# Gradient stages of a test-time-training layer: two gradient products by three float32r passes, silu and tanh in place of the sigmoid, steps written out

## The chip, the cores and the metric

One Trainium2 chip, one of its cores. The metric is the device time of one execution in microseconds, lower is better. Engines: TensorE (PE; PEld is its loading of weights), VectorE (DVE), ScalarE (ACT), GpSimd (POOL), SyncE (SP).

## The reference

Two transformer layers on 4096 tokens of width 128, each attention and a feed-forward part of experts. What the change touches is the second layer's "attention", a test-time-training layer: its parameters gate and val (128x512) and proj (512x128) are improved twice by a gradient over all tokens before they are used.

```python
def loss_fn(p):
    h = jax.nn.swish(k_ttt @ p['gate']) * (k_ttt @ p['val'])
    pred = h @ p['proj']
    return jnp.mean((pred - v_ttt) ** 2)
for _ in range(TTT_STEPS):                      # 2
    grads = jax.grad(loss_fn)(theta)
    theta = {kk: _muon_update(theta[kk], grads[kk]) for kk in theta}
```

With u = k gate, v = k val, s = silu(u), h = s v, dp = pred - v_ttt and dh = dp proj^T, the gradients are dproj = h^T dp, dval = k^T (dh s), dgate = k^T (dh v silu'(u)). silu'(u) = s + sigmoid(u) (1 - s) is called the slope here. `_muon_update` orthogonalizes each gradient (Newton-Schulz), after it is divided by its norm, so a constant factor on one gradient drops out up to rounding.

## The kernel before

The program runs stage by stage, with a barrier between: attention (to 1000 us or so), experts, projection, two rounds of gradient stage (`ttt_grads`) and `newton_schulz` (1323 to 1833 us), then output, routing and the last experts. `ttt_layer` calls the two in turn; both gradient stages run the same code.

`ttt_grads` walks over 32 tiles of 128 tokens. There is no scheduler: each engine's queue is written by hand, and a step n of every queue works on up to four tiles at once, tile n (u, v, s, h), m = n-1 (h transposed, pred, dp), l = n-2 (dp transposed, dh, dwp, du, dv) and o = n-3 (dwg, dwv). 35 steps in all. `steps` (L582) writes out the first four and the last three and makes a hardware loop of the others, four steps a turn. Semaphores count tiles, and every engine works its queue strictly in order.

- TensorE (L1520): transposition of dp (L1534), u and v (L1526, `three_passes`: hi x hi, hi x lo, lo x hi in float32r, which is float32 split into two parts), h transposed in four pieces (L1547), dh (L1526), dwp (L1555), pred (L1563), dwg (L1568), dwv (L1571). dwg, dwv and dwp gather over all tiles in PSUM. dwg and dwv are one float32 product of 128x512 each.
- ScalarE (L1576): the high part of dp^T (L1587), sigmoid of u (L1592), the copy of v (L1596), the copy of h^T (L1601).
- VectorE (L1605): the low part of dp^T (L1617), s = u sg (L1620), the slope in two operations (L1625, L1627), du (L1633), dv (L1634), h (L1639), dp (L1643).
- GpSimd (L1497): the keys of tile n, high and low part, copied from the big transposed array `turned` into `kTs` (L1504); ks, the keys of tile l by rows (L1509); w = slope v (L1515). In its queue the keys of tile n+1 stand behind w of tile n, which waits for VectorE.

The high and low parts of the three trained matrices are made at the start of each stage (L1578 on ScalarE, L1608 on VectorE), and TensorE starts when the last is done. In the trace the name c is the slope's buffer and valw, wv are val.

Of the kernel before, what the change touches and what calls it, by code (L numbers as in the profile page):

```python
# [1462 lines left out]
def ttt_grads(core, keep, grad_ps):  # L1463

# [5 lines left out]
    with ExitStack() as st:  # L1474
        sb = lambda name, shape: [core.sb(st, f"{name}{i}", shape) for i in range(2)]
        parts = lambda name, shape: [core.sb(st, f"{name}_{half}", shape, F32R) for half in ("hi", "lo")]
        kTs, ks = [parts(f"kTs{i}", [P, P]) for i in range(2)], sb("ks", [P, D])
# [4 lines left out]
        u_ps, v_ps, hT_ps, dh_ps = (core.ps(st, n, [P, HID]) for n in ("u_ps", "v_ps", "hT_ps", "dh_ps"))
        pred_ps = core.ps(st, "pred_ps", [P, 2, D])
        names = ("kT_staged", "k_staged", "u_done", "v_done", "sg_ready", "v_copied", "s_ready", "h_ready", "c_ready", "slope_ready", "w_ready",
                 "h_turned", "hT_ready", "pred_done", "dp_ready", "dp_turned", "dpT_ready", "dh_done", "du_ready", "dv_ready",
                 "dwp_done", "dwg_done", "dwv_done", "dpT_hi", "w_hi", "w_lo")
# [1229 lines left out]
```

## Time and profile before

| | us |
|---|---|
| median of 3 runs (lowest, highest) | 2140.37 (2134.65, 2141.48) |
| span of the profiled execution | 2178.4 |
| TensorE busy in it | 1866.1 (86%), 11556 matmuls |
| VectorE busy | 1597.3 (73%) |
| ScalarE busy | 1237.1 (57%) |
| GpSimd busy | 543.2 (25%) |
| mean granted TensorE clock | 0.921 |

The profile is one execution. For that one execution the span, from its first to its last instruction, is the only time given; it lies 38 us above the median of the runs. A timeline row gives the start in us from the span's start, the length in us, the engine, the line, the operation, the tile written and the tiles read, shapes, how many are merged (x8), and in brackets how long the engine sat idle before it and what ended that. Matmuls are pipelined: one row's length runs past the start of the next, so the time an operation costs TensorE is the distance from start to start. "MATMUL ... f32 x8" is four products, each recorded as two. float32r rows are shown with f32 as well; the tiles named _hi and _lo tell them apart.

### The profile page before, as it was taken

Reading aid. Unit: us, or ns where it says so; the run is one execution under the profiler, and the core shown is the slowest. Engines: PE = TensorE matmul, PEld = TensorE weight load, DVE = VectorE, ACT = ScalarE, POOL = GpSimd, SP = SyncE. Lnnn points to the kernel's source line nnn. Section 1 sums busy time; section 2 is a strip of 40 time slices with the busy share of each in tenths; the row PEclk is TensorE's granted clock in tenths of the full one; section 3 lists DMA queues with packets and bytes.
Section 4 is the critical chain, followed back from the end, with each engine's and each line's share of the span. In section 5 each row is a group of like instructions: output and inputs, shape, how many; then the busy total and the mean of one; then the engine's idle time right before and its main releaser. Section 6 shows DMA issues by size and latency. Waiting matters only on the chain. (4 is left out here: it accounts for less than half of the span.)

```text
span 2178.4 us, 35417 instructions
## 1 busy us (share of the span) xinstructions
PE 1866.1 (86%) x11556; PEld 1497.2 (69%) x11556; DVE 1597.3 (73%) x4179; ACT 1237.1 (57%) x2908; POOL 543.2 (25%) x602
## 2 busy tenths in 40 slices
PE   8999999999999999984766486999889998962772
PEld 6888888888888888873656344777667766741662
DVE  7999999999999999976546475777467765767524
ACT  6888888888888888864444363333233322440333
POOL 0111111111111111110544502444034421000472
PEclk9999999999999999996879587999999999985796
DMA  7000000000000000013554100000000000022354
GB/s 226 1 1 1 1 1 1 1 1 1 1 1 1 1 1 1 1 36 56 99 95 105 52 1 1 0 0 0 1 0 0 0 0 5 2 58 87 85 99 92
DMA packets 64893, 61.06 MB, mean 28 GB/s; under 512 B 10698, under 2 KB 54708, under 8 KB 64612
## 3 DMA queue, kind: packets, MB, share of 16 engines
q1 hardware_dynamic: 52276, 41.50, 6.5%
q0 software_dynamic: 10384, 16.59, 4.9%
q8 instruction: 82, 1.34, 0.3%
q10 hardware_dynamic: 2080, 1.05, 0.2%
q14 instruction: 71, 0.58, 0.1%
HBM read 40.12 MB, written 18.73 MB: 27 GB/s over the span
## 5 line engine op out<-in xcount | busy, mean ns | idle before, releaser
L461 DVE TENSOR_TENSOR probT<-turn_ps,probT 128x512 fp32r<-128x512 f32 x512 | 335.3, 686 | 63.3 <-ACT probT L359 63.2
L374 ACT ACTIVATE prob<-prob,negmax 128x512 f32<-128x512 f32 x512 | 375.4, 740 | 4.6 <-DVE negmax L455 4.6
L176 POOL TENSOR_TENSOR x<-x,scaled 128x512 f32<-128x512 f32 x128 | 166.8, 1303 | 802.1 <-DVE scaled L476 802.1
L455 DVE CUSTOM_DVE_ANT_0 prob<-score_ps,bias 128x512 f32<-128x512 f32 x512 | 341.2, 685 | 6.9 <-issue 1.1
L359 ACT CAST probT<-turn_ps 128x512 fp32r<-128x512 f32 x512 | 284.0, 598 | 21.7 <-PE turn_ps L259 21.7
L259 PE MATMUL turn_ps<-ident,prob 128*128 128x128 f32 x2048 | 266.2, 273 | 1.3 <-DVE probT L461 1.1
L276 PE MATMUL work_ps<-probT,val 128*128 128x512 f32 x1024 | 257.2, 393 | 0.1
L259 PEld LDWEIGHTS turn_ps<-ident,prob 128*128 128x128 f32 x2048 | 236.7, 140 | 28.2 <-DVE probT L461 3.4
L247 PE MATMUL score_ps<-k,q 64*128 64x512 f32 x1536 | 213.8, 410 | 2.4 <-DVE negmax L455 2.1
L276 PEld LDWEIGHTS work_ps<-probT,val 128*128 128x128 f32 x1024 | 187.5, 188 | 39.9 <-DVE probT L461 1.7
L247 PEld LDWEIGHTS score_ps<-k,q 64*128 64x128 f32 x1536 | 135.4, 185 | 47.3 <-issue 19.7
L1587 ACT CAST dpT_hi<-pred_ps 128x128 fp32r<-128x128 f32 x64 | 17.1, 267 | 234.1 <-PE pred_ps L1534 234.1
L291 PE MATMUL work_ps<-wo,ctxT 128*128 128x128 f32 x1024 | 146.0, 286 | 0.7 <-ACT ctxT L366 0.7
L291 PEld LDWEIGHTS work_ps<-wo,ctxT 128*128 128x128 f32 x1024 | 123.9, 191 | 26.3 <-issue 22.6
L1515 POOL TENSOR_TENSOR w<-c,vc 128x512 f32<-128x512 f32 x64 | 83.1, 1298 | 207.1 <-DVE c L1627 207.1
L366 ACT COPY ctxT<-work_ps 128x512 f32<-128x512 f32 x128 | 75.1, 587 | 84.5 <-PE work_ps L276 83.4
L374 ACT ACTIVATION_READ_ACCUMULATOR prob<-prob,negmax 128x1 f32 x512 | 106.1, 207 | 0.0
L476 DVE TENSOR_TENSOR scaled<-work_ps,inv 128x512 f32<-128x512 f32 x128 | 87.8, 686 | 2.7 <-PE work_ps L291 2.7
L1620 DVE TENSOR_TENSOR s<-u_ps,sg 128x512 f32<-128x512 f32 x64 | 44.3, 692 | 54.6 <-ACT sg L1592 54.6
L1504 POOL CAST kTs_hi<-turned_hi 128x128 fp32r (+1 forms) x64 | 45.5, 710 | 133.0 <-SPq L1474 133.0
L868 PE MATMUL h_ps<-xgT,own 128*128 128x128 f32 x320 | 60.6, 320 | 14.5 <-issue 14.5
L877 PE MATMUL y_ps<-w,hT 128*128 x320 | 60.6, 319 | 12.7 <-issue 7.2
(510 smaller groups left out, 4010.5 us busy)
## 6 DMA issues: line engine op xcount, KB each, us to landing
ew<-L_ffn_fc_weight SPq DMA_DIRECT2D x32, 256.0 KB
bias<-bias_line SPq DMA_DIRECT2D x16, 448.0 KB, 8.4
mid_rows<-row SPq DMA_DIRECT2D x40, 128.5 KB
last_rows<-row SPq DMA_DIRECT2D x40, 64.0 KB
rows_dram<-qk SPq DMA_DIRECT2D x1, 2304.0 KB, 18.5
x_rows<-x SPq DMA_DIRECT2D x4, 512.0 KB, 7.1
acc_dram<-zero POOLq DMA_DIRECT2D x1, 2048.0 KB, 16.3
out<-x SPq DMA_DIRECT2D x4, 512.0 KB
```

What stands on the lines that cost most here:

```text
L176: pool.tensor_tensor(mine, mine, scaled[a][:, :, :], ALU.add).then_inc(added, 1)
L247: mm = pe.matmul(score_ps[i % 2][a][:, :], q[p % 2][u][head(a), tile_of(i)], k[p % 2][v][head(a), :], start=(n == 0), stop=(n == 2))
L259: mm = pe.transpose(turn_ps[g % 2][:, tile_of(t)], prob[p % 2][a][:, t, tile_of(c)], ident[:, :])
L276: mm = pe.matmul(work[a][:, :], val[p // 2 % 2][:, c, p % 2 * 2 + a, :], probT[n][:, c, :], start=(c == 0 and n == 0), stop=(c == QT - 1 a ...
L291: mm = pe.matmul(work[1][:, tile_of(t)], ctxT[a][:, tile_of(t)], wo[:, 2 * (p % PAIRS) + a, :], start=True, stop=True)
L359: act.copy(probT[0][:, g % QT, :], turn_ps[g % 2][:, :]).then_inc(turned_hi, 1)
L366: act.copy(ctxT[a][:, :], work[a][:, :]).then_inc(ctx_ready, 1)
L374: act.activation(mine, mine, ACT.Exp, bias=negmax[p % 2][:, i, a:a + 1], scale=-1.0, accum_out=total[p % 4][:, i, a:a + 1]).then_inc(exp_d ...
L455: dve.tensor_tensor_reduce(prob[p % 2][a][:, i, :], score_ps[i % 2][a][:, :], bias[:, h, first:first + SEQ][:, ::-1], -1.0, 3.0e38, ALU.ad ...
L461: dve.tensor_tensor(probT[1][:, g % QT, :], turn_ps[g % 2][:, :], probT[0][:, g % QT, :].bitcast(F32), ALU.subtract).then_inc(turned_lo, 1)
L476: dve.tensor_tensor(scaled[a][:, :, :], work[1][:, :].rearrange("p (t d) -> p t d", t=QT), inv[p % 4][:, :, a:a + 1].to_broadcast([P, QT, ...
L1515: pool.tensor_tensor(w[r][:, :], c1[p][:, :], vc[p][:, :], ALU.mult).then_inc(w_ready, 1)
```

## The change

Only `ttt_grads` and one constant of `newton_schulz` change.

1. dwg and dwv are computed by `three_passes` over high and low parts of ks, du and dv. New work: the parts of ks (a cast and a subtraction on GpSimd), the casts of du and dv on ScalarE, the low part of du on VectorE (one step later), the low part of dv on GpSimd.
2. ScalarE computes s = silu(u) and th = tanh(u/2) from PSUM; sigmoid and VectorE's product for s are gone. The slope becomes (s + 1) - (s - 1) th, which is twice silu'(u) (two operations, as before, one step later); the factor 2 on dgate is taken out in `newton_schulz`.
3. The keys' parts are read by TensorE in place; GpSimd's two copies are gone.
4. No hardware loop: all 35 steps are written out. w has two buffers in place of four, and VectorE's order in a step is dpT_lo, du_lo, slope, slope, du, dv, dp, h.
5. u of tile n waits for silu and tanh of tile n-1, v of tile n for the copy of v of tile n-1.

```diff
         @block.gpsimd
-                    for k in range(2):
-                        pool.tensor_copy(kTs[p][k][:, :], kT[k][:, bass.ds(n * P, P)]).then_inc(kT_staged, 1)
+            def keys(l):
+                p = l % 2
+                if l >= 2:
+                    pool.wait_ge(k_lo, l - 1)
+                pool.tensor_tensor(ks[p][:, :], qk[:, l, D:2 * D], keep["shift"][:, D:2 * D], ALU.add).then_inc(k_summed, 1)
+                pool.wait_ge(k_summed, l + 1)
+                if l >= 2:
+                    pool.wait_ge(dwv_done, l - 1)
+                pool.tensor_copy(ks_parts[p][0][:, :], ks[p][:, :]).then_inc(k_hi, 1)
+                pool.wait_ge(k_hi, l + 1)
+                pool.tensor_tensor(ks_parts[p][1][:, :], ks[p][:, :], ks_parts[p][0][:, :].bitcast(F32), ALU.subtract).then_inc(k_lo, 1)
...
+            def low_dv(l):
+                p = l % 2
+                pool.wait_ge(dv_hi, l + 1)
+                if l >= 2:
+                    pool.wait_ge(dwv_done, l - 1)
+                pool.tensor_tensor(dv_parts[p][1][:, :], dv[p][:, :], dv_parts[p][0][:, :].bitcast(F32), ALU.subtract).then_inc(dv_lo, 1)
+
+            for n in range(STEPS):
+                if live(n - 2):
+                    keys(n - 2)
+                if live(n - 1):
+                    weigh_slope(n - 1)
+                if live(n - 2):
+                    low_dv(n - 2)
...
         @block.tensor
-                    pe.wait_ge(kT_staged, 2 * (n + 1))
-                    if again(n, 1):
+                    keys = [half[:, columns(n)] for half in kT]
+                    if n >= 1:
                         pe.wait_ge(s_ready, n)
+                        pe.wait_ge(th_ready, n)
+                    three_passes(u_ps[:, :], keys, wg).then_inc(u_done, 1)
+                    if n >= 1:
                         pe.wait_ge(v_copied, n)
-                    three_passes(u_ps[:, :], kTs[p], wg).then_inc(u_done, 1)
-                    three_passes(v_ps[:, :], kTs[p], wv).then_inc(v_done, 1)
+                    three_passes(v_ps[:, :], keys, wv).then_inc(v_done, 1)
...
-                    pe.matmul(dwg_ps[:, :], ks[q][:, :], du[q][:, :], start=isinstance(o, int) and o == 0,
-                              stop=isinstance(o, int) and o == TILES - 1, skip_group_check=True).then_inc(dwg_done, 1)
+                    pe.wait_ge(k_lo, o + 1)
+                    pe.wait_ge(du_lo, o + 1)
+                    three_passes(dwg_ps[:, :], whole(ks_parts[o % 2]), du_parts[o % 2], **edges).then_inc(dwg_done, 1)
+                    pe.wait_ge(dv_lo, o + 1)
+                    three_passes(dwv_ps[:, :], whole(ks_parts[o % 2]), dv_parts[o % 2], **edges).then_inc(dwv_done, 1)
...
         @block.scalar
-                    act.activation(sg[p][:, :], u_ps[:, :], ACT.Sigmoid).then_inc(sg_ready, 1)
+                    act.activation(s[r][:, :], u_ps[:, :], ACT.Silu).then_inc(s_ready, 1)
+                    if n >= 2:
+                        act.wait_ge(c_ready, n - 1)
+                    act.activation(th[p][:, :], u_ps[:, :], ACT.Tanh, scale=0.5).then_inc(th_ready, 1)
...
+                if live(l):
+                    p = l % 2
+                    act.wait_ge(du_ready, l + 1)
+                    if l >= 2:
+                        act.wait_ge(dwg_done, l - 1)
+                    act.copy(du_parts[p][0][:, :], du[p][:, :]).then_inc(du_hi, 1)
+                    act.wait_ge(dv_ready, l + 1)
+                    if l >= 2:
+                        act.wait_ge(dwv_done, l - 1)
+                    act.copy(dv_parts[p][0][:, :], dv[p][:, :]).then_inc(dv_hi, 1)
...
         @block.vector
-                    dve.tensor_tensor(s[r][:, :], u_ps[:, :], sg[p][:, :], ALU.mult).then_inc(s_ready, 1)
+                if live(o):
+                    p = o % 2
+                    dve.wait_ge(du_hi, o + 1)
+                    if o >= 2:
+                        dve.wait_ge(dwg_done, o - 1)
+                    dve.tensor_tensor(du_parts[p][1][:, :], du[p][:, :], du_parts[p][0][:, :].bitcast(F32), ALU.subtract).then_inc(du_lo, 1)
...
+                    dve.scalar_tensor_tensor(c1[p][:, :], s[r][:, :], -1.0, th[p][:, :], ALU.add, ALU.mult).then_inc(c_ready, 1)
+                    dve.wait_ge(c_ready, m + 1)
+                    dve.scalar_tensor_tensor(c1[p][:, :], s[r][:, :], 1.0, c1[p][:, :], ALU.add, ALU.subtract).then_inc(slope_ready, 1)
...
-                act.activation(first[m], x_ps[m], ACT.Copy, scale=grad_scale).then_inc(copied, 1)
+                act.activation(first[m], x_ps[m], ACT.Copy, scale=grad_scale * (0.5 if m == 0 else 1.0)).then_inc(copied, 1)
```

The order of instructions, at the places that matter. TensorE, the end of a step, from pred on; before:

```order
L1563 MATMUL pred_ps<-proj,hT_460 128x128 x4
L1568 MATMUL dwg_ps<-du_468,ks_434 128x512
L1571 MATMUL dwv_ps<-dv_470,ks_434 128x512
L1534 MATMUL pred_ps<-ident,dp_462 128x128
L1536 ISA
L1526 MATMUL u_ps<-wg_hi,kTs_hi 128x512
```

and now (`turned` is the array with the transposed keys):

```order
L1578 MATMUL pred_ps<-proj,hT_458 128x128 x4
L1539 MATMUL dwg_ps<-du_hi,ks_hi 128x512
L1539 MATMUL dwg_ps<-du_lo,ks_hi 128x512
L1539 MATMUL dwg_ps<-du_hi,ks_lo 128x512
L1539 MATMUL dwv_ps<-dv_hi,ks_hi 128x512
L1539 MATMUL dwv_ps<-dv_lo,ks_hi 128x512
L1539 MATMUL dwv_ps<-dv_hi,ks_lo 128x512
L1547 MATMUL pred_ps<-ident,dp_460 128x128
L1539 MATMUL u_ps<-wg_hi,turned_hi 128x512
```

Two products became six passes; nothing else moved on TensorE. GpSimd, one step, before:

```order
L1504 COPY kTs_hi<-turned_hi 128x128
L1504 COPY kTs_lo<-turned_lo 128x128
L1509 TENSOR_TENSOR ks_434<-qk,shift 128x128
L1515 TENSOR_TENSOR w_458<-c_446,vc_444 128x512
```

and now:

```order
L1501 TENSOR_TENSOR ks_430<-qk,shift 128x128
L1505 CAST ks_hi<-ks_430 128x128
L1507 TENSOR_TENSOR ks_lo<-ks_430,ks_hi 128x128
L1514 TENSOR_TENSOR w_455<-c_445,vc_443 128x512
L1521 TENSOR_TENSOR dv_lo<-dv_468,dv_hi 128x512
```

and VectorE's step now:

```order
L1641 TENSOR_TENSOR dpT_lo<-pred_ps,dpT_hi 128x128
L1647 TENSOR_TENSOR du_lo<-du_465,du_hi 128x512
L1654 SCALAR_TENSOR_TENSOR c_445<-s_449,th_441 128x512
L1656 SCALAR_TENSOR_TENSOR c_445<-s_449,c_445 128x512
L1661 TENSOR_TENSOR du_466<-dh_ps,w_456 128x512
L1664 TENSOR_TENSOR dv_468<-dh_ps,s_448 128x512
L1667 TENSOR_TENSOR dp_459<-pred_ps,v 128x128
L1673 TENSOR_TENSOR h_454<-s_450,vc_444 128x512
```

GpSimd has a second 128x512 operation in each step; VectorE has eight operations as before, h now last. ScalarE, from the start of the stage, now:

```order
L1591 CAST wpT_hi<-projT 128x512
L1605 ACT_TABLE_LOAD
L1605 ACTIVATE s_447<-u_ps 128x512
L1608 ACTIVATE th_441<-u_ps 128x512
L1612 COPY vc_443<-v_ps 128x512
L1605 ACTIVATE s_448<-u_ps 128x512
L1608 ACTIVATE th_442<-u_ps 128x512
L1612 COPY vc_444<-v_ps 128x512
L1617 COPY hT_457<-hT_ps 128x512
```

One table load stands ahead of the first silu, where one stood ahead of the first sigmoid; no other follows before the square root of Newton-Schulz.

## Rows read from the trace of the kernel before

**Rows 1.** Windows: length, busy of PE, PEld, DVE, ACT, POOL, clock, DMA share, GB/s
```profile
1323.00:1336.00 13.00, 5.83 (x13) 4.04 (x14) 5.16 (x8) 4.72 (x7) 2.64 (x5) 0.50 0.00 1
...
1396.00:1426.00 30.00, 30.00 (x169) 23.12 (x168) 22.10 (x40) 9.73 (x20) 12.91 (x19) 1.00 0.00 0
```
**Rows 2.** Timeline of one middle step, TensorE (start, length, operation, shapes)
```profile
1401.93 0.27 PE L1534 MATMUL pred_ps<-ident,dp 128*128 128x128 f32 x1
...
1402.75 0.39 PE L1526 MATMUL v_ps<-wv_hi,kTs_hi 128*128 128x512 f32 x1
...
1403.44 0.60 PE L1547 MATMUL hT_ps<-ident,h 128*128 128x128 f32 x4
...
1403.79 0.48 PE L1526 MATMUL dh_ps<-wpT_hi,dpT_hi 128*128 128x512 f32 x1
1404.11 0.39 PE L1526 MATMUL dh_ps<-wpT_lo,dpT_hi 128*128 128x512 f32 x1
...
1405.46 1.06 PE L1563 MATMUL pred_ps<-proj,hT 128*128 128x128 f32 x8
...
1406.35 1.02 PE L1568 MATMUL dwg_ps<-du,ks 128*128 128x512 f32 x2
...
1408.07 0.27 PE L1534 MATMUL pred_ps<-ident,dp 128*128 128x128 f32 x1
```
**Rows 3.** Timeline of the same step, the other engines
```profile
1402.31 0.46 POOL L1509 TENSOR_TENSOR ks<-qk,shift 128x128 f32<-128x128 f32 x1 [0.45 <-PE dwv_ps L1571]
...
1402.70 0.29 DVE L1617 TENSOR_TENSOR dpT_lo<-pred_ps,dpT_hi 128x128 fp32r<-128x128 f32 x1 [1.03 <-ACT dpT_hi L1587]
1402.95 0.60 ACT L1592 ACTIVATE sg<-u_ps 128x512 f32<-128x512 f32 x1 [0.36 <-PE u_ps L1526]
...
1404.15 0.59 ACT L1601 COPY hT<-hT_ps 128x512 f32<-128x512 f32 x1
...
1405.80 1.27 POOL L1515 TENSOR_TENSOR w<-c,vc 128x512 f32<-128x512 f32 x1 [3.04 <-DVE c L1627]
...
1406.84 0.78 DVE L1639 TENSOR_TENSOR h<-s,vc 128x512 f32<-128x512 f32 x1
1407.02 0.75 POOL L1504 CAST kTs_hi<-turned_hi 128x128 fp32r x1
...
1407.55 0.28 DVE L1643 TENSOR_TENSOR dp<-pred_ps,v 128x128 f32<-128x128 f32 x1
```
**Rows 4.** Timeline of the start of the first gradient stage
```profile
1323.79 0.62 ACT L1578 CAST wg_hi<-gate 128x512 fp32r<-128x512 f32 x1 [5.23 <-PEq L59]
...
1324.32 0.61 ACT L1578 CAST wv_hi<-valw 128x512 fp32r<-128x512 f32 x1
1324.44 0.69 DVE L1608 TENSOR_TENSOR wg_lo<-gate,wg_hi 128x512 fp32r<-128x512 f32 x1 [5.09 <-ACT wg_hi L1578]
...
1325.47 1.28 ACT L1592 ACT_TABLE_LOAD   x1
...
1328.08 0.60 ACT L1592 ACTIVATE sg<-u_ps 128x512 f32<-128x512 f32 x1 [1.33 <-PE u_ps L1526]
...
1330.77 0.68 DVE L1639 TENSOR_TENSOR h<-s,vc 128x512 f32<-128x512 f32 x1
1330.94 1.64 POOL L1515 TENSOR_TENSOR w<-c,vc 128x512 f32<-128x512 f32 x1 [6.60 <-DVE c L1627]
...
1333.10 0.79 PE L1526 MATMUL u_ps<-wg_hi,kTs_hi 128*128 128x512 f32 x1 [3.78 <-POOL kTs_lo L1504]
...
1340.02 0.48 PE L1534 MATMUL pred_ps<-ident,dp 128*128 128x128 f32 x1 [0.38 <-DVE dp L1643]
```
**Rows 5.** Timeline of GpSimd at the span's start
```profile
1.25 0.28 POOL L165 TENSOR_SCALAR_AFFINE_SELECT ident<-ident 128x128 f32<-128x128 f32 x1 [0.24 <-POOL ident L163]
```
**Rows 6.** Timeline of the end of the second gradient stage
```profile
1785.03 0.68 DVE L1634 TENSOR_TENSOR dv<-dh_ps,s 128x512 f32<-128x512 f32 x1
...
1787.69 1.02 PE L1571 MATMUL dwv_ps<-dv,ks 128*128 128x512 f32 x2
```

More of the change, by code:

```diff
@@ L1476, in ttt_grads @@
         parts = lambda name, shape: [core.sb(st, f"{name}_{half}", shape, F32R) for half in ("hi", "lo")]
-        kTs, ks = [parts(f"kTs{i}", [P, P]) for i in range(2)], sb("ks", [P, D])
+        two_parts = lambda name, shape: [parts(f"{name}{i}", shape) for i in range(2)]
+        ks, ks_parts = sb("ks", [P, D]), two_parts("ks", [P, D])
         wg, wv, wpT = (parts(n, [P, HID]) for n in ("wg", "wv", "wpT"))
-        sg, vc, c1 = (sb(n, [P, HID]) for n in ("sg", "vc", "c1"))
-        s, h, w = ([core.sb(st, f"{n}{i}", [P, HID]) for i in range(RING)] for n in "shw")
@@ L1481, in ttt_grads @@
-        hT, dp, dpT, du, dv = sb("hT", [P, HC, P]), sb("dp", [P, D]), [parts(f"dpT{i}", [P, P]) for i in range(2)], sb("du", [P, HID]), sb("dv", [P, HID])
+        th, vc, c1 = (sb(n, [P, HID]) for n in ("th", "vc", "c1"))
+        s, h = ([core.sb(st, f"{n}{i}", [P, HID]) for i in range(RING)] for n in "sh")
+        w = sb("w", [P, HID])
+        hT, dp, dpT = sb("hT", [P, HC, P]), sb("dp", [P, D]), two_parts("dpT", [P, P])
+        du, dv, du_parts, dv_parts = sb("du", [P, HID]), sb("dv", [P, HID]), two_parts("du", [P, HID]), two_parts("dv", [P, HID])
@@ L1490, in ttt_grads @@
+        (k_summed, k_hi, k_lo, u_done, v_done, s_ready, th_ready, v_copied, h_ready, c_ready, slope_ready, w_ready,
+         h_turned, hT_ready, pred_done, dp_ready, dp_turned, dpT_hi, dpT_ready, dh_done, du_ready, dv_ready,
+         du_hi, dv_hi, du_lo, dv_lo, dwp_done, dwg_done, dwv_done, w_hi, w_lo) = (core.sem(n) for n in names)
         block = st.enter_context(nc.Block())
-        run = lambda eng, step: steps(eng, step, TILES, 3, RING, RING)
-        live = lambda n: not isinstance(n, int) or 0 <= n < TILES
@@ L1522, in _, with three_passes @@
             pe.wait_ge(w_lo, len(trained))
-            def three_passes(to, left, right):
+            def three_passes(to, left, right, start=True, stop=True, across=False):
                 for k, (i, j) in enumerate(PASSES):
-                    mm = pe.matmul(to, left[i][:, :], right[j][:, :], start=(k == 0), stop=(k == 2))
+                    mm = pe.matmul(to, left[i], right[j][:, :], start=start and k == 0, stop=stop and k == 2, skip_group_check=across)
                 return mm
-            def step(n, r):
-                p, q = r % 2, 1 - r % 2
+            whole = lambda two: [half[:, :] for half in two]
+            for n in range(STEPS):
                 m, l, o = n - 1, n - 2, n - 3
@@ L1578, in _ @@
                 act.copy(hi[:, :], whole[:, :]).then_inc(w_hi, 1)
-            def step(n, r):
-                p, q = r % 2, 1 - r % 2
+            for n in range(STEPS):
                 m, l = n - 1, n - 2
```

123 lines of the change are left out of this document (52 added, 71 removed).

## Prediction

> **What bounds the kernel now.** The busy shares of the page are averages over stages with different limits, so the table by stage comes first [rows 1]: in 30 us from the middle of a gradient stage TensorE is busy for 30.00 at a granted clock of 1.00 (its 2.4 GHz level), VectorE for 22.10, GpSimd for 12.91, ScalarE for 9.73. TensorE sets the pace there. The timeline of one step, TensorE alone, shows it [rows 2]: from one transposition of dp (1401.93) to the next (1408.07) are 6.14 us, and each operation starts where the one before it ends. The reader should see a belt: transposition and u 0.82 (to 1402.75), v 0.69, transpositions of h 0.35, dh and dwp 1.67, pred 0.89, dwg and dwv 1.72; together 6.14. The other engines in the same step [rows 3] have gaps: the dp that TensorE takes at 1408.07 is ready at 1407.83, and w and the copy of h^T lie well ahead of their readers.
>
> **TensorE, steady state.** The change replaces dwg and dwv, float32 operations that take 1.72 together (1406.35 to 1408.07 [rows 2]), by three float32r passes each. v is three such passes of 128x512 in 0.69 (1402.75 to 1403.44), so 0.23 each. The first pass behind a float32 operation took 0.32 (dh, 1403.79 to 1404.11); six passes take 6 x 0.23 = 1.38, or 1.47 if that 0.09 is paid once, behind pred. The gain is 0.25 to 0.34 a step. I take the middle, 0.30, since dwg also stands behind a float32 operation but its weights are small and may be loaded during pred: a step takes 5.84. Of a stage's steps three fill and three drain, counted below; 29 steps x 0.30 = 8.7 us in a stage.
>
> **What must stay hidden for that.** I lay a step of 5.84 out from the durations of the rows, time 0 being the transposition of dp.
> ScalarE: silu can start where sigmoid does now (1.02) and ends at 1.62; neither a row for silu nor for tanh exists, the bounds are a copy of the same size from PSUM (0.59) and the cast from SBUF (0.62), and I take the 0.60 of sigmoid. Tanh starts 0.53 later (the spacing of the casts wg_hi and wv_hi [rows 4]), then the copies of v and h^T, the last one to 3.25. pred may start at 3.53, as in the belt: 0.3 in hand, where today there are 0.7 (copy ends at 1404.74, pred starts at 1405.46 [rows 2, 3]). The casts of du and dv, 0.62 each as wg_hi, follow du and dv, to 5.3.
> VectorE: the product for s leaves (0.69, as long as its neighbours), du_lo comes (0.69, as wg_lo<-gate,wg_hi [rows 4]). dpT_lo goes to 0.97 as now, du_lo to 1.8, the two slope operations to 3.4, du to 4.0, dv to 4.6, dp when pred is done, 4.66 to 4.94, h to 5.6. TensorE wants dp at 5.84: 0.9 in hand.
> GpSimd: the two copies of keys leave (the first takes 0.75 [rows 3]), as TensorE reads them in place. The cast and the low part of ks come (0.28 as the select of 128x128 [rows 5], 0.46 as ks), and the low part of dv. No row has a two-input float32r output on GpSimd: the lower bound is w's 1.27 for as many elements, the upper one w's 1.64 under VectorE's h [rows 4]; I take 1.27, which is the same shape undisturbed. Sum 0.46 + 0.28 + 0.46 + 1.27 + 1.27 = 3.74, and twice 0.24 between operations that depend on each other [rows 5]: 4.2 of 5.84. dv_lo is ready near 6.7, and its reader, dwv, stands at 5.84 + 5.2: hidden with 4 us in hand. If that cover were gone, each step would grow by what it is late.
> The shared port: GpSimd and VectorE hold each other off when VectorE has two inputs in SBUF. h is issued 1.04 behind w and takes 0.78 in place of 0.68; kTs_hi, issued under h, takes 0.75 [rows 3] where the select of its size takes 0.28 [rows 5]; w takes 1.64 in place of 1.27 when issued 0.17 behind h [rows 4]. So w keeps VectorE out for 1.04 + 0.10 = 1.14, and h keeps GpSimd out for 0.17 + 0.37 = 0.54. In the new step du_lo, both slope operations and h are of that kind, 4 x 0.54 = 2.16. Laid out: ks 0.73 to 1.19, its cast behind du_lo at 1.63, its low part behind the first slope operation, 2.38 to 2.84, w behind the second, 3.5 to 4.8, under du and dv, which read PSUM, h from 4.87, dv_lo from 5.4 to 6.7, 0.83 into the next step, when its ks is due. It closes, with a few tenths in hand. I take 0; below 0 is excluded, since TensorE's belt is full, and above it stands rival (c).
>
> **Filling and draining.** Today u of tile 1 stands at 1333.10, because its staged keys were queued on GpSimd behind w of tile 0 [rows 4]. With keys in place it waits for tanh of tile 0: 1328.08 + 0.53 + 0.60 = 1329.2, 3.9 earlier, with the same work behind it up to the first transposition of dp (1340.02 today). The clock was 0.50 here [rows 1]. If it rises at the same moment as today, the work that moves forward is done more slowly and 1 is given back; if it rises as early as the work does, 2 are won. Range 3 to 6, taken 4.0. At the end, du and dv of the last tile get casts and low parts: dv at 1785.03 + 0.68, cast 0.62, GpSimd 1.3, three passes 0.69, to 1788.4; today's last dwv starts at 1787.69 and needs 0.86, to 1788.55 [rows 6]. No change. Casts, low parts and the table load at the start of a stage stay.
>
> **Sum.** 2 x (8.7 + 4.0) = 25.4 us. The profiled execution has a span of 2178.4, so it should show 2153. The median of the runs lies 38 lower (2140.4), and no row ties that difference to these stages, so the gain is carried over whole: 2140.4 - 25.4 = 2115.
>
> **Rivals.**
> (a) Half of the 0.30 is refilled, because the copy of h^T comes later than planned and pred waits, and a step takes 6.0: 2 x (29 x 0.14 + 4) = 16, 2124. For it: the 0.3 in hand there is the smallest of all. Chance 0.14.
> (b) All of it is refilled and a step stays at 6.14: only the filling is won, 8, which gives 2132. Chance 0.10.
> (c) Slower: the port. Should dv_lo get in ahead of h (its input is there at 5.3, h starts at 4.87, so half a microsecond decides), GpSimd keeps VectorE out for 1.14 in every step, besides 0.33 + 0.15 + 0.33 for the operations on ks (each 0.13 less than its length, as w). VectorE's loop is 0.67 from the transposition to the start of dpT_lo, 0.2 + 0.6 + 0.7 + 0.6 + 0.6 + 0.6 + 0.3 from there through dp, some 4.4 with the way back; with 1.95 of exclusion 6.3, with part of h in it 6.6. GpSimd's own sum says alike: 4.2 + 2.16 = 6.3 with nothing overlapped. From 6.37 a step the kernel is slower by over 0.3%; at 6.6 it is 2 x (29 x 0.46 - 4) = +19: 2159. Against it: the layout closes. Chance 0.12, slower GpSimd operations included. The Trainium skill has this as a rule, in "SBUF — State Buffer", section "SBUF: two separate sides": of a GpSimd operation and a VectorE operation with two SBUF inputs the one that starts first has the shared pair for the whole instruction, and the other blocks. The trace agrees (0.10 on h, 0.47 on kTs_hi).
> (d) The change does not do what it says: silu and tanh share no function table, and each tile pays two loads, 64 x 2 x 1.28 = 164 [rows 4]: 2279. Against it: the program has one load a stage, ahead of the first silu. Chance 0.02. The Trainium skill ("ScalarE: Activation LUTs", section "Table sets: the hidden batching unit") lists tanh beside exp and beside sigmoid, names no set for silu, and says to group calls by set. The instruction order shown above says that here they share one.
>
> **How the numbers follow.** My forecast has 0.62: with 0.25 a step and 3 of filling it gives 20.5 (2120), with 0.34 and 6 it gives 31.7 (2109). About 0.3% (6.4 us) is what a measurement can tell from no change, so faster is below 2134. Faster: 0.62 + 0.14 + half of (b) = 0.81. Same: the rest of (b) and a little of (c), 0.07. Slower: 0.12. The range runs from 2107 (2 below the best end, for the scatter of the runs, which is 7 wide) through (a) and (b) to 2135; (c) and (d) are outside.
>
> **What would show it.** Right: TensorE busy 30.00 of 30.00 in mid-stage, transpositions of dp 5.8 to 5.9 apart, six passes of 0.23 where 1.72 stood, the last dwv some 25 us ahead of 1787.69, one table load a stage, u of tile 1 about 3 us behind u of tile 0. Wrong, by step: TensorE idle ahead of pred for h^T (a); idle ahead of the transposition for dp, with h or du_lo far above 0.69, or w and dv_lo above 1.3 (c); u of tile 1 still late (filling). If steps are 5.8 apart and the time has not fallen, the loop written out costs elsewhere.

## The result and the profile after

| | before | after |
|---|---|---|
| median (lowest, highest), 4 runs each | 2137.51 (2132.53, 2141.48) | 2105.76 (2104.53, 2107.28) |
| span of the profiled execution | 2178.4 | 2102.6 |
| length of the two gradient stages in it | 212.8, 211.9 | 195.2, 195.0 |
| mean granted TensorE clock | 0.921 | 0.933 |

The ratio is 0.9854, 95% interval 0.9839 to 0.9869: 31.7 us less, where the prediction had 25.4. (The kernel before has one run more than when the prediction was made, and its median came 2.9 lower.) A stage's length is taken here from its first cast to ScalarE's first reading of dwg. The two stages are 34.4 shorter together (424.65 to 390.23). The spans differ by 75.8, but 43.1 of that lies ahead of the first gradient stage (its first cast at 1280.69, 1323.79 before [rows 4]), in code that the change leaves alone: in the trace of before, GpSimd idles 38.8 us at the experts' gathers for VectorE, in the one after 8.1, which is 30.7 of the 43.1. That is no part of the gain, and below only stage lengths and ratios are compared between runs.

The page of the changed kernel (busy time and share, instructions):

```profile
PE 1828.0 (87%) x11684; PEld 1508.8 (72%) x11684; DVE 1603.9 (76%) x4179; ACT 1338.7 (64%) x3100; POOL 705.4 (34%) x666
```

The windows that answer to [rows 1], start and middle of a stage:

```profile
1280.00:1293.00 13.00, 8.32 (x33) 6.12 (x34) 5.77 (x11) 7.55 (x14) 2.96 (x4) 0.72 0.00 1
1353.00:1383.00 30.00, 30.00 (x187) 26.19 (x186) 23.55 (x42) 18.17 (x36) 27.00 (x27) 1.00 0.00 1
```

TensorE still sets the pace, with no gap. GpSimd rose from 12.91 to 27.00 of 30 and is the next in line. At the start the clock is 0.72 where it was 0.50. One middle step, TensorE, answering to [rows 2]:

```profile
1360.13 0.27 PE L1547 MATMUL pred_ps<-ident,dp 128*128 128x128 f32 x1
...
1363.65 1.06 PE L1578 MATMUL pred_ps<-proj,hT 128*128 128x128 f32 x8
...
1364.46 0.48 PE L1539 MATMUL dwg_ps<-du_hi,ks_hi 128*128 128x512 f32 x1
...
1364.78 0.39 PE L1539 MATMUL dwg_ps<-du_lo,ks_hi 128*128 128x512 f32 x1
...
1365.01 0.39 PE L1539 MATMUL dwg_ps<-du_hi,ks_lo 128*128 128x512 f32 x1
...
1365.92 0.27 PE L1547 MATMUL pred_ps<-ident,dp 128*128 128x128 f32 x1
```

From transposition to transposition are 5.79 (6.14 before). The six passes take 1.46 (1364.46 to 1365.92) in place of 1.72, and pred 0.81 in place of 0.89. The other engines in the same step, answering to [rows 3]:

```profile
1360.94 0.68 DVE L1647 TENSOR_TENSOR du_lo<-du,du_hi 128x512 fp32r<-128x512 f32 x1
1360.96 0.99 POOL L1501 TENSOR_TENSOR ks<-qk,shift 128x128 f32<-128x128 f32 x1
1361.13 0.60 ACT L1605 ACTIVATE s<-u_ps 128x512 f32<-128x512 f32 x1 [0.43 <-PE u_ps L1539]
...
1361.54 0.95 DVE L1654 SCALAR_TENSOR_TENSOR c<-s,th 128x512 f32<-128x512 f32 x1
1361.63 0.59 ACT L1608 ACTIVATE th<-u_ps 128x512 f32<-128x512 f32 x1
...
1362.57 0.61 ACT L1617 COPY hT<-hT_ps 128x512 f32<-128x512 f32 x1
...
1363.50 1.27 POOL L1514 TENSOR_TENSOR w<-c,vc 128x512 f32<-128x512 f32 x1
...
1364.74 0.29 DVE L1667 TENSOR_TENSOR dp<-pred_ps,v 128x128 f32<-128x128 f32 x1 [0.33 <-PE pred_ps L1578]
...
1364.95 0.68 DVE L1673 TENSOR_TENSOR h<-s,vc 128x512 f32<-128x512 f32 x1
...
1365.15 1.64 POOL L1521 TENSOR_TENSOR dv_lo<-dv,dv_hi 128x512 fp32r<-128x512 f32 x1 [0.38 <-ACT dv_hi L1627]
```

The copy of h^T ends at 1363.18, 0.47 ahead of pred; dp is there at 1365.03, 0.89 ahead of its transposition. GpSimd and VectorE pay for their shared port in what they have to spare: ks 0.99 (0.46 alone), the slope's first operation 0.95 (0.69 alone), dv_lo 1.64 (least 1.27). The start of the first stage, answering to [rows 4]:

```profile
1282.37 1.28 ACT L1605 ACT_TABLE_LOAD   x1
...
1283.29 0.80 PE L1539 MATMUL u_ps<-wg_hi,turned_hi 128*128 128x512 f32 x1 [8.56 <-DVE wpT_lo L1633]
...
1285.47 0.59 ACT L1608 ACTIVATE th<-u_ps 128x512 f32<-128x512 f32 x1
...
1286.21 0.77 PE L1539 MATMUL u_ps<-wg_hi,turned_hi 128*128 128x512 f32 x1
1286.26 0.59 ACT L1612 COPY vc<-v_ps 128x512 f32<-128x512 f32 x1 [0.20 <-PE v_ps L1539]
...
1286.77 0.62 PE L1539 MATMUL u_ps<-wg_lo,turned_hi 128*128 128x512 f32 x1
...
1287.69 0.40 PE L1539 MATMUL v_ps<-wv_lo,turned_hi 128*128 128x512 f32 x1
```

u of tile 1 stands 2.92 behind u of tile 0, with no idle time of TensorE ahead of it, and the copy of v of tile 0 starts only then. At about 1287 the passes go from 0.43 apart to 0.23: the clock rose from 0.50 to 1.00 3.8 after u of tile 0; before, it rose some 14.5 after.

### The profile page after: what moved, and what is told of

The parts are those of the page before. It is cut to its first block and busy times, and to the rows that moved or that the text cites. A ratio compares the mean times of both kernels' runs of the same rounds, so it can differ in the third digit from the quotient of the medians.

```text
span 2102.6 us, 35597 instructions
## 1 busy us (share of the span) xinstructions
PE 1828.0 (87%) x11684; PEld 1508.8 (72%) x11684; DVE 1603.9 (76%) x4179; ACT 1338.7 (64%) x3100; POOL 705.4 (34%) x666
## 3 DMA queue, kind: packets, MB, share of 16 engines
q10 hardware_dynamic: 2080, 1.05, 0.2%
## 5 line engine op out<-in xcount | busy, mean ns | idle before, releaser
L1521 POOL TENSOR_TENSOR dv_lo<-dv,dv_hi 128x512 fp32r<-128x512 f32 x64 | 102.1, 1596 | 27.4 <-ACT dv_hi L1627 27.4
L1623 ACT CAST du_hi<-du 128x512 fp32r<-128x512 f32 x64 | 39.6, 619 | 51.3 <-DVE du L1661 51.3
L1570 PEld LDWEIGHTS dwp_ps<-dp,h 128*128 128x128 f32 x512 | 67.2, 191 | 5.6
L1578 PE MATMUL pred_ps<-proj,hT 128*128 128x128 f32 x512 | 67.8, 275 | 2.0 <-ACT hT L1617 2.0
L1570 PE MATMUL dwp_ps<-dp,h 128*128 128x128 f32 x512 | 67.6, 275 | 0.0
```

Of the source, the lines that this page charges most:

```text
L1521: pool.tensor_tensor(dv_parts[p][1][:, :], dv[p][:, :], dv_parts[p][0][:, :].bitcast(F32), ALU.subtract).then_inc(dv_lo, 1)
L1570: mm = pe.matmul(dwp_ps[:, c, :], h[l % RING][:, columns(c)], dp[l % 2][:, :], start=l == 0 and c == 0, stop=l == TILES - 1, skip_group_ch ...
```

## The experiments

They ran on four chips: b_out, b_keys, a_f32 and a_swap, where the kernel before took 2136.91 (19 runs); b_keys_h, a_sig, a_pool1 and a_pool2 (2143.59, one run); b_keys_v, a_vwait, a_warm and a_start (2178.12, 7 runs); b_keys_vd, after_5 and a_start_5 (2188.14, 9 runs). On the last two the first gradient stage begins 42 to 55 us later than in the trace of after, with GpSimd waiting at the gathers named above (43.0 us in after_5). So the table gives what the traces show of the stages themselves, first / second stage, in us: the length; u of tile 1 and the transposition of dp of tile 0 (T0) and of tile 1 (T1), counted from u of tile 0; and the mean step of tiles 4 to 28. The changed kernel itself, on two chips, differs by 0.7 and 0.8 in its stages (after, after_5), 0.6 and 0.4 of it ahead of T0; a difference of that size between two chips' traces is not a finding.

| | length | u1 | T0 | T1 | step |
|---|---|---|---|---|---|
| before | 212.8 / 211.9 | 6.71 / 6.52 | 13.63 / 12.52 | 20.08 / 19.18 | 6.143 |
| after | 195.2 / 195.0 | 2.92 / 2.73 | 8.02 / 7.79 | 13.05 / 12.83 | 5.793 |
| b_out | 212.4 / 212.7 | 6.70 / 6.70 | 12.60 / 12.45 | 19.88 / 20.03 | 6.141 |
| b_keys | 208.2 / 208.3 | 3.69 / 3.70 | 9.66 / 9.67 | 15.66 / 15.69 | 6.140 |
| b_keys_h | 210.1 / 208.2 | 3.69 / 3.70 | 10.58 / 9.67 | | 6.146 |
| b_keys_v | 206.9 / 206.4 | 3.06 / 2.40 | 8.32 / 7.71 | 14.32 / 13.71 | 6.143 |
| b_keys_vd | 205.6 / 205.3 | 3.06 / 2.73 | 7.99 / 7.66 | 13.28 / 12.95 | 6.133 |
| a_f32 | 205.2 / 205.2 | 2.91 / 2.88 | 7.81 / 7.77 | 12.84 / 12.80 | 6.133 |
| a_swap | 196.4 / 196.0 | | | | 5.793 |
| a_sig | 208.4 / 208.5 | 3.05 | 7.98 / 8.08 | 13.5 | 6.190 |
| a_pool1 | 195.1 / 195.0 | | | | 5.793 |
| a_pool2 | 203.2 / 203.4 | | | | 6.042 |
| a_vwait | 199.2 / 198.8 | 3.70 / 3.69 | 10.58 / 10.58 | 16.56 / 16.17 | 5.803 |
| a_warm | 195.1 / 194.5 | 2.90 / 2.24 | 7.56 / 6.86 | 12.59 / 11.89 | 5.793 |
| a_start | 193.7 / 193.6 | 2.85 / 2.92 | 7.46 / 7.54 | 12.49 / 12.56 | 5.793 |
| after_5 | 195.9 / 195.9 | 2.91 / 2.91 | 8.62 / 8.22 | 13.64 / 13.25 | 5.793 |
| a_start_5 | 194.1 / 193.9 | 2.89 / 2.81 | 7.83 / 7.42 | 12.86 / 12.45 | 5.793 |

### Parts alone and parts undone

**b_out**: the kernel before, its loop written out.

```diff
-        run = lambda eng, step: steps(eng, step, TILES, 3, RING, RING)
+        run = lambda eng, step: [step(n, n % RING) for n in range(TILES + 3)]
```

> The kernel before with the hardware loop written out and nothing else. Theory A: turning the loop costs nothing that a full TensorE shows, so steps 6.14, a stage 212 to 213, the time within 3 us of the kernel before. Rival (the loop's branches cost something every four steps, which was part of the gain): a stage 1 to 5 us shorter.

Measured 2135.18, ratio 0.9987 (0.9977 to 0.9997), stages and step as before. The medians are 1.7 us apart, a little beyond the noise, but the gradient stages, where the loop stood, are no shorter: there it cost nothing.

**b_keys**: b_out with the keys read in place.

```diff
-                    for k in range(2):
-                        pool.tensor_copy(kTs[p][k][:, :], kT[k][:, bass.ds(n * P, P)]).then_inc(kT_staged, 1)
...
-                    pe.wait_ge(kT_staged, 2 * (n + 1))
```

> The kernel before with two things of the change alone: the steps are written out, and TensorE reads the keys in place (GpSimd's two copies and the wait for them are gone). Theory A (the filling was mis-sized: TensorE starts tile 1 at once, so it is busier and its clock rises early): u of tile 1 stands 3 to 3.5 us behind u of tile 0 in place of 6.7, the second transposition of dp 6 to 7 us earlier than in the kernel before counted from u of tile 0, steps still 6.14, a stage 206 in place of 212.8, the time 12 to 14 us below the kernel before. Rival B (the surplus came from the steps, or from silu and tanh on ScalarE, and the keys only win the 4 us that were taken): second transposition 3.5 to 4 earlier, a stage 209, the time 8 lower.

2128.94, ratio 0.9965 (0.9952 to 0.9978): 8.0 us, 4.0 a stage, what the prediction took for it, and no more. So rival B held; theory A's early start did not come, as u of tile 1 stands at 3.69 and not at 3 to 3.5. Against b_out on the same chip, which has the loop written out too, the medians are 6.2 apart and the stages in the traces 8.7.

**a_f32**: the changed kernel with dwg and dwv in float32 again, without casts and low parts.

```diff
-                    three_passes(dwg_ps[:, :], whole(ks_parts[o % 2]), du_parts[o % 2], **edges).then_inc(dwg_done, 1)
+                    pe.matmul(dwg_ps[:, :], ks[o % 2][:, :], du[o % 2][:, :], start=o == 0, stop=o == TILES - 1, skip_group_check=True).then_inc(dwg_done, 1)
```

> The changed kernel with dwg and dwv as float32 products again (no casts and low parts of ks, du, dv); silu, tanh, keys in place and the order of VectorE stay. Theory A: steps of 6.14 again, filling as in the changed kernel, a stage 195.2 + 31 x 0.345 = 206, the time 21 us above the changed kernel and some 13 below the kernel before. Rival B: if the 0.345 a step has another source than the passes, steps stay near 5.8 to 5.9.

2125.36, ratio 0.9944 (0.9928 to 0.9961), step 6.133. The passes are worth 0.34 a step and 10 a stage. But a_f32 is also 3.05 a stage shorter than b_keys, 2.8 to 2.9 of it ahead of T1. The prediction has no term for that; b_keys_h and the group "The missing filling" look for it.

**a_swap**: dv and its cast ahead of du, so that dv_lo gets its input before h starts, as rival (c) wanted.

```diff
                     dve.wait_ge(dh_done, l + 1)
-                    dve.wait_ge(w_ready, l + 1)
-                    dve.tensor_tensor(du[p][:, :], dh_ps[:, :], w[p][:, :], ALU.mult).then_inc(du_ready, 1)
                     if l >= 2:
                         dve.wait_ge(dv_lo, l - 1)
                     dve.tensor_tensor(dv[p][:, :], dh_ps[:, :], s[l % RING][:, :], ALU.mult).then_inc(dv_ready, 1)
+                    dve.wait_ge(w_ready, l + 1)
+                    dve.tensor_tensor(du[p][:, :], dh_ps[:, :], w[p][:, :], ALU.mult).then_inc(du_ready, 1)
...
```

> The changed kernel with dv ahead of du on VectorE and its cast ahead on ScalarE, so that dv_lo on GpSimd is ready to go 0.6 earlier, ahead of h. Theory A (VectorE has 0.9 in hand and h is needed late): h takes up to 1.8 in place of 0.68, steps stay 5.79 to 5.85, the time within 4 us of the changed kernel. Rival (c) of the prediction (the port decides when dv_lo gets in ahead of h): steps 6.3 to 6.6, a stage 16 to 25 us longer, the time 30 to 50 us above the changed kernel.

2103.26, ratio 0.9843 (0.9824 to 0.9862), step 5.793. The two tiles in its trace (duration ns least/median/most):

```profile
L1521 POOL TENSOR_TENSOR dv_lo<-dv,dv_hi x64: 1268/1291/1848, 1296.4 to 1710.1; 128x512 fp32r<-128x512 f32 x64
...
L1673 DVE TENSOR_TENSOR h<-s,vc x64: 683/1409/1829, 1287.2 to 1700.8; 128x512 f32<-128x512 f32 x64
```

The collision happens: h takes 1.41 where it took 0.68, and dv_lo no longer waits (1.29 for 1.64). It costs no step anything; VectorE's spare time takes it up (26.86 busy of 30 in mid-stage, for 23.55). The stages are 1.2 and 1.0 longer all the same: 0.7 of that lies behind the last transposition of dp, where TensorE idles 1.17 for du_lo, now made later, and the rest ahead of T0. Rival (c)'s place was right and its price was not.

### What is next in line

**b_keys_h**: b_keys with h of tile n ahead of the slope's operations on VectorE.

```diff
                 if live(n):
+                    dve.wait_ge(v_copied, n + 1)
+                    if again(n, RING):
+                        dve.wait_ge(dwp_done, n - RING + 1)
+                    dve.tensor_tensor(h[r][:, :], s[r][:, :], vc[p][:, :], ALU.mult).then_inc(h_ready, 1)
```

> The kernel with keys in place and steps written out (b_keys), and VectorE's h moved ahead of the two slope operations. Theory A (what the prediction left out of the filling is that h of a tile no longer stands behind two slope operations, 1.4 us): first transposition of dp 8.2 to 8.4 behind u of tile 0 in place of 9.7, a stage 206 to 207 in place of 208.2, steps 6.14. Rival B (the filling got shorter because silu on ScalarE makes s at once, without VectorE): first transposition stays within 0.5 of 9.7, a stage 208.

2129.0 in one run, the stages no shorter than b_keys's; the first is 1.9 longer, and the clock rises only 12.6 after u of tile 0 in it. That theory of the missing 3 us fell.

**a_sig**: the changed kernel with the sigmoid on ScalarE and the product for s on VectorE again.

```diff
-                    act.activation(s[r][:, :], u_ps[:, :], ACT.Silu).then_inc(s_ready, 1)
-                    act.activation(th[p][:, :], u_ps[:, :], ACT.Tanh, scale=0.5).then_inc(th_ready, 1)
+                    act.activation(th[p][:, :], u_ps[:, :], ACT.Sigmoid).then_inc(th_ready, 1)
...
+                    dve.tensor_tensor(s[n % RING][:, :], u_ps[:, :], th[n % 2][:, :], ALU.mult).then_inc(s_ready, 1)
```

> The changed kernel with sigmoid and VectorE's product for s again (s just ahead of h, at the end of VectorE's step), the slope in its old form; passes, keys and casts as in the change. Theory A: u of tile 1 waits for s of VectorE and stands 3.7 behind u of tile 0 in place of 2.9, the filling is 1 to 2 us longer, steps stay 5.79 to 5.85 because VectorE's ninth operation fits, a stage 196 to 198. Rival B (silu and tanh are needed for the step: VectorE has nine operations, 5.0 us, and up to 1.2 of waiting for the port): steps of 6.0 to 6.4, a stage 202 or more.

**a_pool1** and **a_pool2**: the changed kernel with one more copy a step on GpSimd that nobody reads, 128x128 and 128x512.

```diff
+                    pool.wait_ge(more_done, n - 1)
+                    pool.tensor_copy(more[n % 2][:, :], wp[:, :, :].rearrange("p a b -> p (a b)")).then_inc(more_done, 1)
```

> The changed kernel with one more copy of 128x128 on GpSimd in each step, behind w. GpSimd is busy for 5.3 of 5.79 in the changed kernel, waiting for the port included; the copy takes 0.3 to 0.65. Theory A (TensorE sets the step, GpSimd is next with 0.5 in hand): steps 5.79 to 5.85. Rival (c) of the prediction (the port ring is already at its limit): steps 6.1 or more.

> The changed kernel with one more copy of 128x512 on GpSimd in each step, behind w. Theory A: GpSimd's queue, with 0.5 in hand, becomes the longest and each step grows by the copy's length less 0.5: steps 6.0 to 6.5, a stage 7 to 22 us longer. Rival: the copy is hidden, steps 5.79, because waiting for the port shrinks by as much.

One run each: a_sig 2126.04, a_pool1 2105.33, a_pool2 2123.07. The middle window of a_sig, then of a_pool2:

```profile
1353.00:1383.00 30.00, 29.39 (x177) 24.12 (x176) 29.66 (x44) 15.35 (x30) 23.69 (x25) 1.00 0.00 1
```

```profile
1353.00:1383.00 30.00, 29.81 (x180) 24.67 (x179) 29.83 (x40) 17.39 (x35) 29.28 (x31) 1.00 0.00 1
```

With the product for s back on VectorE, VectorE is busy 29.66 of 30, a step takes 6.19, and the whole gain of the passes is gone, as rival B had it (u of tile 1 stood at 3.05, not at theory A's 3.7). So in a steady step silu and tanh save nothing on a path of their own; they make the room in which the low part of du is free. Another place for that product in VectorE's queue was not tried. In a_pool2 a copy that takes 0.60 undisturbed, and 1.08 in a middle step, lengthens the step by 0.25: GpSimd had under a microsecond to spare (a_pool1's copy fits in), and VectorE is busy 29.83 with the same eight operations. du, dv and dp, which read PSUM, are as long as before; the four with both inputs in SBUF now wait longer for the port:

```profile
1359.36 1.72 POOL L1522 TENSOR_TENSOR dv_lo<-dv,dv_hi 128x512 fp32r<-128x512 f32 x1
...
1359.86 1.77 DVE L1657 SCALAR_TENSOR_TENSOR c<-s,th 128x512 f32<-128x512 f32 x1
```

The slope's first operation takes 1.77, for 0.95 in the changed kernel and 0.69 alone. That is the ring of rival (c): it closes one 128x512 copy beyond this change.

### The missing filling

**b_keys_v** and **a_vwait**: one wait of TensorE moved, forward in b_keys and back in the changed kernel. In b_keys_v

```diff
                         pe.wait_ge(s_ready, n)
-                        pe.wait_ge(v_copied, n)
                     three_passes(u_ps[:, :], here, wg).then_inc(u_done, 1)
+                    if again(n, 1):
+                        pe.wait_ge(v_copied, n)
```

and in a_vwait

```diff
                         pe.wait_ge(th_ready, n)
+                        pe.wait_ge(v_copied, n)
                     three_passes(u_ps[:, :], keys, wg).then_inc(u_done, 1)
-                    if n >= 1:
-                        pe.wait_ge(v_copied, n)
```

> b_keys with one wait of TensorE moved: the wait for the copy of v of tile n-1 stands ahead of v of tile n, no longer ahead of u. Theory A (part of the 3 us a stage that b_keys still lacks in filling is this wait: TensorE idles 0.77 ahead of u of tile 1, and the clock rises later): no gap there, u of tile 1 within 3.0 of u of tile 0 (3.69 in b_keys), passes at 0.23 by 5 us behind u of tile 0, first transposition of dp at 8.0 to 8.8 (9.66), stage 206 to 207 (208.2). The rest of the 3 us would be VectorE's queue ahead of dp. Theory B (the wait is nothing, since sigmoid and s of tile 0 are late as well): u of tile 1 stays at 3.4 or more, stage 208.2. Steps 6.14 by both.

> The changed kernel with the wait for the copy of v of tile n-1 put back ahead of u of tile n. Theory A: u of tile 1 some 0.7 later (3.6 behind u of tile 0, 2.9 in the changed kernel), the clock rises later, first transposition of dp at 9 to 9.7 (8.0), stage 196.3 to 197.2 (195.1). Theory B: stage within 0.3 of 195.1. Step 5.79 by both.

One run each, 2170.77 and 2150.8. b_keys_v is 1.2 and 1.9 a stage shorter than b_keys; a_vwait is 4.0 and 3.7 longer than after and 3.3 and 2.9 longer than after_5, more than any theory expected. TensorE at the start of a_vwait, the wait's gap first, then pred of tile 0:

```profile
1329.51 0.77 PE L1539 MATMUL u_ps<-wg_hi,turned_hi 128*128 128x512 f32 x1 [0.77 <-ACT vc L1611]
...
1333.93 2.08 PE L1577 MATMUL pred_ps<-proj,hT 128*128 128x128 f32 x8 [0.67 <-ACT hT L1616]
```

and its windows from u of tile 0 on, then the changed kernel's:

```profile
1325.80:1329.80 4.00, 3.22 (x7) 2.15 (x8) 0.33 (x1) 2.04 (x4) 0.00 (x0) 0.50 0.00 0
1329.80:1333.80 4.00, 3.46 (x10) 2.37 (x9) 1.66 (x3) 2.18 (x4) 2.08 (x4) 0.50 0.02 4
1333.80:1337.80 4.00, 3.48 (x12) 3.00 (x13) 1.48 (x4) 0.35 (x2) 0.36 (x1) 0.50 0.00 0
1337.80:1341.80 4.00, 4.00 (x27) 3.54 (x26) 2.28 (x4) 2.88 (x6) 1.29 (x1) 0.91 0.00 0
```

```profile
1283.20:1287.20 4.00, 3.91 (x9) 2.67 (x10) 0.28 (x2) 2.12 (x4) 0.00 (x0) 0.50 0.00 0
1287.20:1291.20 4.00, 2.72 (x17) 2.06 (x15) 1.98 (x5) 2.05 (x4) 2.00 (x4) 0.99 0.00 0
```

The wait itself is 0.77 of idle time (3.22 busy of 4.00, 3.91 without it). The rest is the clock: it stays at 0.50, its 1.2 GHz level, through twelve us instead of four, pred takes 2.08 where the same eight products take 1.16 in the changed kernel's first step, and T0 comes at 10.58 in place of 8.02. How late the clock rises varies: from u of tile 0 it is 11.9 and 12.7 in a_vwait's two stages, 7.7 and 8.1 in those of b_keys with the same gap, and 3.5 to 6.0 without the gap (after, after_5, a_f32, a_swap, a_pool1, a_pool2). So in each pair of kernels the wait costs more than its 0.77, but how much more is not settled by single runs.

**b_keys_vd**: b_keys_v with VectorE's dp ahead of h, as in the changed kernel.

> b_keys_v with VectorE's dp ahead of h, as the changed kernel has it. Theory A (what b_keys_v still lacks is dp queued behind h in filling: in it dp of tile 1 starts a microsecond behind the end of pred): transposition of dp of tile 1 about 5.3 behind that of tile 0 (6.0 in b_keys_v), stage 205 to 205.9, the level of a_f32 (205.2). Theory B (h comes too late for its transposition, or the order of the two is nothing): 6.0 and 206.4 to 207.0 as in b_keys_v. Steps 6.14 by both.

2169.08 in one run. The stages are 1.3 and 1.05 shorter. Of that 0.71 lies between T0 and T1, which go from 6.00 to 5.29 apart in both stages; the rest is smaller than what chips differ by. VectorE at that point, in b_keys_v and in b_keys_vd:

```profile
1338.71 0.78 DVE L1635 TENSOR_TENSOR h<-s,vc 128x512 f32<-128x512 f32 x1
...
1339.41 0.28 DVE L1639 TENSOR_TENSOR dp<-pred_ps,v 128x128 f32<-128x128 f32 x1
```

```profile
1344.78 0.28 DVE L1634 TENSOR_TENSOR dp<-pred_ps,v 128x128 f32<-128x128 f32 x1
1344.97 0.68 DVE L1639 TENSOR_TENSOR h<-s,vc 128x512 f32<-128x512 f32 x1
```

In the middle of a stage this order costs next to nothing, since dp is early (steps of 6.143 and 6.133); in filling TensorE waits for dp. With both edits a stage is 205.3 to 205.6, against 205.2 in a_f32: the account closes within 0.4, less than one kernel's stages differ between chips. The traces show where most of that is, in the wait for dp ahead of T1, in b_keys_vd and then in a_f32:

```profile
1345.11 0.33 PE L1529 MATMUL pred_ps<-ident,dp 128*128 128x128 f32 x1 [0.64 <-DVE dp L1634]
```

```profile
1301.96 0.33 PE L1539 MATMUL pred_ps<-ident,dp 128*128 128x128 f32 x1 [0.38 <-DVE dp L1643]
```

In b_keys_vd VectorE works without a pause from the product for s through the slope, du and dv to dp; in a_f32, where silu has made s and the slope is a step later, it idles ahead of dp for pred. That is 0.26 a stage for item 2 of the change, read from the traces and not made alone by an edit.

**a_warm** and **a_start**: the changed kernel with the start of the stage altered. a_warm puts 14 transpositions of the identity ahead of TensorE's first wait; a_start puts 8, and lets u of tile 0 wait for gate's low part alone.

```diff
+            keep_busy(pe, hT_ps, ident, 8)
-            pe.wait_ge(w_lo, len(trained))
...
+                    if n == 0:
+                        pe.wait_ge(w_lo, 1)
                     three_passes(u_ps[:, :], keys, wg).then_inc(u_done, 1)
```

> The changed kernel with 14 transpositions of the identity on TensorE at the start of each gradient stage, while it waits for the parts of the trained matrices; their result is never read. If the clock's level at the start is what filling still costs: passes of u of tile 0 at 0.23 instead of 0.43, stage 1 to 1.5 shorter (193.6 to 194.1), time 2 to 3 lower than the changed kernel's, 2103. If the level falls again before u of tile 0, or filling is bound by the chain of small operations rather than by TensorE: stage 194.8 to 195.2, 2105.5.

> The changed kernel with 8 such transpositions, and with the one wait for all low parts of the trained matrices taken apart: u of tile 0 waits for gate's, v for val's, dh for proj's. u of tile 0 can start about 1.2 earlier. If both count: stage 1.2 to 2.5 shorter (192.6 to 193.9), time 2101 to 2103.5. If the sigmoid-side chain behind v of tile 0 sets the filling: stage 194.5 or more, 2105.

a_warm: 2145.14, ratio 0.9842 (0.9817 to 0.9866); a_start: 2146.44, ratio 0.9849 (0.9822 to 0.9876). The first four us of a_warm's first stage from u of tile 0 on, after 2.9 us of transpositions with no gap behind them:

```profile
1329.80:1333.80 4.00, 4.00 (x13) 2.70 (x12) 0.33 (x1) 1.82 (x5) 0.00 (x0) 0.62 0.00 0
```

Here the passes of u of tile 0 stay 0.43 apart, which theory had at 0.23: that was a miss. In its second stage they are at 0.23 from the start, though TensorE idled 0.86 behind the transpositions:

```profile
1565.22 0.50 PE L1540 MATMUL u_ps<-wg_hi,turned_hi 128*128 128x512 f32 x1 [0.86 <-DVE wpT_lo L1634]
1565.56 0.40 PE L1540 MATMUL u_ps<-wg_lo,turned_hi 128*128 128x512 f32 x1
1565.80 0.40 PE L1540 MATMUL u_ps<-wg_hi,turned_lo 128*128 128x512 f32 x1
```

In the changed kernel, too, the second stage begins with the clock at 1.00, which Newton-Schulz left; but TensorE idles up to its first pass, and the level falls to 0.50 within half a microsecond of it (in after_5 it had fallen 1.7 ahead of it). In no run without transpositions did it last through the first microsecond. With them it stayed at 1.00 in the second stage of a_warm and of a_start_5, and fell in that of a_start. So a filler may keep the level, and did not raise it ahead of the first passes in any first stage. a_warm's stages are 0.1 to 0.5 shorter than those of after, 0.8 to 1.4 shorter than those of after_5, so whether the filler is worth anything in all stays open. a_start's, where u of tile 0 starts 1.0 and 1.2 earlier, are 1.4 to 2.3 shorter than either. To see whether that reaches the total, both kernels ran beside each other on another chip:

> The changed kernel again, as the control for the run beside it on the same chip. Ratio to the kernel before 0.984 to 0.987.

> a_start again, beside the changed kernel on one chip. Its stages are 1.4 shorter in the trace, so 2.8 less than the control if nothing is given back between the stages (ratio 0.0013 lower); if Newton-Schulz or the barrier gives it back: within 1 of the control.

after_5: 2151.57 (2146.80 to 2153.71), ratio 0.9831 (0.9811 to 0.9852): 36.6 us less than before where the first chip had 31.7, and a ratio just below the 0.984 expected. a_start_5: 2150.24 (2149.57 to 2153.41), ratio 0.9827 (0.9807 to 0.9847). The stages are 1.8 and 2.0 shorter in the trace, the medians differ by 1.3 and the runs overlap: no version was shown to beat the changed kernel.

## Where the prediction held, and which step failed

- **The bound** (TensorE's belt, 30.00 of 30.00) and **what stays hidden**: right. The layout held nearly in every place: the copy of h^T 0.47 ahead of pred where 0.3 was forecast, dp 0.89 in hand where 0.9 was, dv_lo behind h, GpSimd with a few tenths to spare (a_pool1, a_pool2). Rivals (a) and (b) did not come about.
- **Steady state**, "I take the middle, 0.30": it was 0.35, just beyond the upper end of 0.34. Where the prediction weighed whether 0.09 would be paid behind pred, the trace shows both: the first pass takes 0.32 to the next, as dh's did, and pred becomes 0.08 shorter when a float32r pass follows it. The whole of pred, dwg and dwv went from 2.61 to 2.27. That the weights of dwg are small was no reason for less: dwg's first pass took what dh's did. By this 0.05 x 29 x 2 = 2.9 us were missed.
- **Filling**: "the same work behind it up to the first transposition of dp" is the step that failed. The start of u of tile 1 was right to 0.1 (3.8 earlier, 3.9 forecast), and b_keys alone gave the 4.0 a stage taken. But the changed kernel's filling gave 7.2 (7.6 and 6.7 from before to a_f32): T0 came 5.6 and 4.7 earlier, and T1 another 1.4 and 1.6. The other 3 are two items of the change's description that the prediction priced at nothing without saying so: the wait for the copy of v, moved from u to v (1.2 and 1.9 a stage in b_keys_v), and VectorE's order, dp ahead of h (1.3 and 1.05 in b_keys_vd). Of the 0.4 and 0.15 left, the wait ahead of T1 shows 0.26 for item 2, s ready without VectorE; the remainder is within what chips differ by. The term's range of 3 to 6 took the clock as the only unknown and so was too narrow.
- **The sum** by traces: keys 8.2, the moved wait 3.1, dp ahead of h 2.4, the rest of the filling 0.6, passes 20.1, together 34.4. It closes because each term is the difference of two traces; b_keys_v and b_keys_vd ran once each, and on other chips. The medians' 31.7 is below that; its interval, 28 to 34, takes it in just about, and after_5's 36.6 lies above, so which is nearer isn't settled. The result, 2105.76, lies 1.2 below the range.
- **Drain**, no change: right, from the last transposition of dp to the reading of dwg are 6.56 before and 6.57 after, though TensorE idles 0.21 there for dv_lo.
- **Rival (c)**: its collision was made in a_swap and costs no step anything at this load; in a_pool2, one copy later, a step grows. Its step from which the kernel is slower, 6.37, should be 6.39 by its own formula. The Trainium skill ("SBUF — State Buffer", section "SBUF: two separate sides") has the shared pair go to whichever operation starts first, for the whole instruction, with the other blocked. The traces agree (h goes from 0.68 to 1.41 behind dv_lo), but here the price in a step was zero until the loser's slack was used up. **Rival (d)**: one load of 1.28 a stage, for 32 silu and 32 tanh; they share a set. **Loop**: nothing (b_out).
- The profiled span was forecast as 2153 and came as 2102.6. That the 38 us between before's profiled execution and its median belonged to the stages outside was right; that the next profiled execution would show them again was not.

## What to carry to other kernels

Price filling as a chain of its own: list which wait ends last at each of the first tiles, and treat every moved wait and every swapped pair in an engine's queue as a term there, even where the steady state hides it fully. A short idle of TensorE while its clock is low costs more than its length, so take such a wait off the first matmuls first. And count what a cheaper operation on one engine makes room for: the silu on ScalarE shortens little itself (0.26 a stage), yet without it the faster products were worth nothing: a_sig's stages of 208.4 are 3 us longer than b_keys_vd's, which has float32 products and the sigmoid.

## What the runs showed of the hardware that was not expected

- 0.77 us of idle time behind the first six passes came with a later rise of the clock in all six stages that have it: 7.7 to 12.7 us after the first pass (b_keys, b_keys_h, a_vwait) in place of 3.5 to 6.0 in twelve stages without it. It cost 3 to 4 us a stage in a_vwait and 1.2 to 1.9 in b_keys against b_keys_v. Within one kernel the rise moved from 7.7 to 12.6 between stages (b_keys_h); how it is decided is left open.
- With transpositions ahead of the first passes a clock that stood at 1.00 stayed there in two of three second stages (a_warm, a_start_5, not a_start), and in none without them; 2.9 us of them did not raise a low one in time in the first stage of a_warm.
- pred takes 0.81 when a float32r pass follows it and 0.89 when a float32 product does (after, a_f32), while the first float32r pass behind it costs 0.09 more than the next ones (0.32 and 0.23).
- On GpSimd a float32r output costs nothing extra: dv_lo undisturbed takes 1.27, as w. A copy of 128x512 there takes 0.60 undisturbed and 1.08 in the middle of a_pool2.
